# Attention scores of the array's two halves issued one by one instead of in pairs

## The chip, the cores and the metric

The kernel runs on one core of one Trainium2 chip. The metric is the device time of one execution in microseconds. A core has TensorE (PE in the profile; its weight loads are PEld), VectorE (DVE), ScalarE (ACT), GpSimd (POOL) and SyncE (SP), each with its own queue of instructions in order. They meet at semaphores. Matmuls write to PSUM, which has 8 banks of 512 fp32 columns on 128 partitions.

## The reference

One transformer layer with post-normalisation on x of 1024 tokens by 512:

```python
q = x @ Wq                      # 32 heads of 16
k, v = split(x @ Wkv)           # 8 groups of 16; 4 heads share a group
scores = q @ k.T                # causal: keys after the query are -inf
weights = softmax(scores / 4)
ctx = weights @ v
x = layernorm(x + ctx @ Wo + bo)
x = layernorm(x + x @ W.T + bias + lora(x))   # 8 adapters of rank 16, weighted
```

## The kernel before

**Units and cycles.** The sequence is cut into two halves of 512 queries (HT), and a unit is one half with one group: 4 heads, 16 units (NU). A unit's work on scores, exponentials and values is cut into *cycles*: one cycle takes 256 queries (s) and 256 keys, that is two key blocks of 128 (p). The first half has 3 cycles per unit, the second 7; 80 cycles in all. Cycle 24 is the first of the second half, and from there on the work repeats after two units, 14 cycles.

**Halves of the array.** A score matmul needs only 48 or 51 rows of the 128 (fp32 split in three terms of 16 rows, and three rows that carry the negated maximum). So two heads' pairs lie on two halves of the array's rows, partitions 0 to 63 and 64 to 127 (`tile_rows(t, ...)`, t = 0 or 1, PAIR = 2). Two matmuls that use different halves and different banks can run together.

**Pieces.** In each cycle, scores are computed in four *pieces*, each one bank: key block 0 on halves 0 and 1, then key block 1 on halves 0 and 1. The diagonal's second block is only 256 wide. The pieces' bank is `score_bank(e)`: three banks (3, 4, 5) go round up to piece 284 (cycle 71), six after that. ScalarE takes the exponential of each piece (L845) into PB. `bank_free(e)` makes TensorE wait until the exponential three pieces back is done. `accumulate(cyc - 1)` (L1300) then multiplies the previous cycle's probabilities by the values, in 16 small matmuls on bank 6. On diagonal cycles GpSimd masks PB first (L700).

**Chunks.** The maximum of each row must be known before the exponential, so the scores are also computed ahead with queries on the partitions: a *chunk* is one bank of such scores (L1118), for one block of 128 queries and one or two heads. VectorE reads it: a plain maximum where all keys are allowed (L897), or with the causal mask added (L904). 320 chunks in all, alternating between the array's halves: chunk n is on half n % 2. They use banks 0 to 2, and bank 7 when nothing else holds it; `CHUNK_BEHIND[n]` names the chunk or job that had the bank before, and `was_read` waits until it was read. When a unit's chunks are done, its maxima go through GpSimd, TensorE (`turn_maxima`, L1126), ScalarE and a DMA into three extra rows of QS, before the unit's first cycle.

**Order.** Everything is in an order written out ahead. The projections run first as jobs in three parts (`PLAN_A`), with the first 16 chunks between the parts. Then `DUE[c]` says how many chunks are due before cycle c; `level` computes it from costs, so that chunks are spread by the room that a cycle leaves on TensorE and VectorE. `chunks_of_cycle` cuts a cycle's lot in four quarters. TensorE's order within a cycle is: quarter 0, the pair of pieces 0 and 1, quarter 1, quarter 2, the pair of pieces 2 and 3, quarter 3, the cycle's *filler* if it has one, then `accumulate` of the cycle before. Fillers (`FILL`) are the late projections (Q, WE), transposes of the finished context (T1a, T1b, T2, T3) and the two output products (WO, FF). VectorE reads the chunks in the same order and does its part of the fillers after quarter 0. After cycle 79 a tail works off the last four blocks of tokens.

**Waits.** `max_scores` and `scores` each have one semaphore, raised once per pair by the last matmul of the pair. VectorE waits for pair n // 2 of `max_scores`, ScalarE for pair e // 2 of `scores`. SyncE waits for `scores` before it loads a new unit's queries into a slot of QS (5 slots, `load_queries`).

Of the kernel before, what the change touches and what calls it, by code (L numbers as in the profile page):

```python
# [18 lines left out]
def postln_kernel(nc, x, wq, wkv, wo, bo, lora_a, lora_b, w, bias, lora_w, xt, out):  # L19
# [120 lines left out]
    def chunks_of_job(n, part):  # L140

        before, due = PLAN_A[n - 1][1] if n else 0, PLAN_A[n][1]
        a, b = (before + (due - before) // 2 * p // 3 * 2 for p in (part, part + 1))
        return range(a, b)
# [48 lines left out]
    def level(chunks, cycles):  # L193

        total = COST[chunks[-1] + 1] - COST[chunks[0]]
        low, high = 0.0, 9.0
        for _ in range(40):
            ratio = (low + high) / 2
            room = [max(0.0, ratio * (0.4 * pe_time(c) + 1500) - 0.7 * dve_time(c)) for c in cycles]
            low, high = (low, ratio) if sum(room) > total else (ratio, high)  # L200
        done, due = 0.0, []
        for r in room:
            done += r
            due.append(2 * sum(1 for n in chunks[::2] if COST[n + 2] - COST[chunks[0]] <= done + 1))
        due[-1] = len(chunks)
        return [chunks[0] + d for d in due]
# [12 lines left out]
    def chunks_of_cycle(c):  # L219

        lot = range(DUE[c], DUE[c + 1])
        return [lot[len(lot) // 2 * q // 4 * 2:len(lot) // 2 * (q + 1) // 4 * 2] for q in range(4)]

# [70 lines left out]
    with ctx:  # L294
# [97 lines left out]
        qs_in = [sem(f"qs_in{s}") for s in range(SLOTS)]  # L392
        max_scores = sem("max_scores")
        max_read = sem("max_read")
# [4 lines left out]
        nm_in = sem("nm_in")  # L399
        scores = sem("scores")  # L400
        probs = sem("probs")
# [63 lines left out]
        def _(sp):  # L465
# [35 lines left out]
            def load_queries(u):  # L501
# [4 lines left out]
                if u >= SLOTS:  # L506
                    sp.wait_ge(scores, SCORE_BANKS[FIRST[u - SLOTS + 1]] // PAIR)
                parts_landed(PROJ.index(("Q", h, c)))
# [206 lines left out]
        def _(act):  # L715
# [120 lines left out]
            for cyc in range(NCYC):  # L836
# [4 lines left out]
                for k, (_, heads, skip) in enumerate(pieces(cyc)):  # L841
                    e = SCORE_BANKS[cyc] + k
                    width = len(heads) * (HQ - skip)
                    act.wait_ge(scores, e // PAIR + 1)
                    nc.scalar.activation(PB[:, cyc % NP_BUF, k, 0:width], PS[:, score_bank(e), 0:width], ACT.Exp,  # L845
# [35 lines left out]
        def _(dve):  # L881
# [7 lines left out]
            def chunk_max(n):  # L889
# [4 lines left out]
                bank = PS[:, CHUNK_BANK[n], :]  # L894
                dve.wait_ge(max_scores, n // PAIR + 1)
                if not own:
# [191 lines left out]
        def _(pe):  # L1088
# [7 lines left out]
            def chunk_scores(n):  # L1096

                u, qb, own, _ = CHUNKS[n]
                h, v = divmod(u, G)
# [12 lines left out]
                was_read(CHUNK_BEHIND[n])  # L1112
                was_read(CHUNK_BEHIND[n + 1])
                for k in range(len(CHUNKS[n][3])):
                    for t in range(PAIR):
                        j = CHUNKS[n + t][3][k]
                        rows = tile_rows(t, ROWS)
                        last = nc.tensor.matmul(PS[:, CHUNK_BANK[n + t], k * width:(k + 1) * width],  # L1118
                                                QS[rows, u % SLOTS, j % NPAIR, qb * P:(qb + 1) * P],
                                                KS[rows, v // 2, k0:k0 + width], start=True, stop=True)  # L1120
                last.then_inc(max_scores, 1)

# [134 lines left out]
            for n in range(NJOB_A):  # L1257
                for part in range(3):
                    pe_job(n, part)
                    for k in chunks_of_job(n, part)[::PAIR]:  # L1260
                        chunk_scores(k)
                    if JOBS[n] == ("V", 0, 0) and part == 1:
                        direct_queries()
                    if JOBS[n] == ("V", 1, 0) and part == 1:
                        turn_maxima(0)
# [52 lines left out]

            def pair_scores(cyc, i):

                u, s, _ = CYCLES[cyc]
                kb = key_blocks(cyc)[i]
                e = SCORE_BANKS[cyc] + PAIR * i
                for t in range(PAIR):
                    bank_free(e + t)
                for t in range(PAIR):
                    _, heads, skip = pieces(cyc)[PAIR * i + t]
                    rows = tile_rows(t, NROW)
                    last = nc.tensor.matmul(PS[:, score_bank(e + t), 0:len(heads) * (HQ - skip)],  # L1329
                                            KS[rows, (u % G) // 2, kb * P:(kb + 1) * P],  # L1330
                                            QS[rows, u % SLOTS, :, s * HQ + skip:(s + 1) * HQ], start=True, stop=True)
                last.then_inc(scores, 1)

            for cyc, (u, _, _) in enumerate(CYCLES):
                if cyc == FIRST[u]:
                    pe.wait_ge(nm_in, 16 * PAIR * (u + 1))
                for j, lot in enumerate(chunks_of_cycle(cyc)):
                    for n in lot[::PAIR]:
                        chunk_scores(n)
                    if j % 2 == 0:  # L1340
                        pair_scores(cyc, j // 2)
                    if cyc == rows_cycle(1) + 1 and j == 0:
                        turn_maxima(1)
                    filler(cyc, j)
# [73 lines left out]
```

## Time and profile before

| | us |
|---|---|
| median of 3 runs | 417.46 |
| lowest and highest run | 415.34, 418.66 |
| the profiled execution | 416.12 |
| its span in the profile | 414.4 |
| TensorE matmul busy | 337.4 (81%) |
| VectorE busy | 258.2 (62%) |
| ScalarE busy | 215.4 (52%) |
| GpSimd busy | 129.3 (31%) |

The span is the time from the first to the last instruction of the one profiled execution; its own measured time is 1.7 us longer. Matmuls are pipelined, so TensorE's busy time counts a matmul's latency too, and a share under 100% doesn't measure how much room is left. The idle time before an instruction is given with what ended it. The granted clock of TensorE was 0.887 of full speed on average over the span.

### The profile page before, as it was taken

What the parts mean: (1) busy time and instruction counts of PE and PEld (TensorE: products, weight loads), DVE (VectorE), ACT (ScalarE), POOL (GpSimd) and SP (SyncE); (2) the same over time, 40 slices, a digit from 0 to 9 for tenths busy, and PEclk for the clock granted to TensorE, in tenths of its full rate; (3) what the DMA queues carried; (4) which work ended last, traced back from release to release, by engine and by line L of the source; (5) the groups of instructions that cost most, each with busy time, mean ns of one, the idle gap of its engine ahead of it and who ended that gap; (6) DMA issues with size and microseconds to landing.
All of it is one profiled execution on the core that took longest, in us unless ns stands there. A gap on an engine that the chain in (4) does not pass through costs nothing.

```text
span 414.4 us, 7602 instructions
## 1 busy us (share of the span) xinstructions
PE 337.4 (81%) x2495; PEld 190.5 (46%) x2495; DVE 258.2 (62%) x783; ACT 215.4 (52%) x438; POOL 129.3 (31%) x292
## 2 busy tenths in 40 slices
PE   7986787877878887987878777788877876989994
PEld 3754454553543434433434434344343533546883
DVE  3455639457576556677687766878667775105664
ACT  4522425426345456566564755737647555595241
POOL 8730213222233335444512211321014112232353
PEclk9988568869897557599999989999899998899999
DMA  7766153832242101101001000000000000000002
GB/s 235 257 190 182 33 171 102 217 93 70 74 143 95 48 3 43 38 2 42 1 5 38 27 14 29 2 4 25 5 0 2 5 25 2 3 2 27 0 2 103
DMA packets 14198, 24.41 MB, mean 59 GB/s; under 512 B 2064, under 2 KB 4880, under 8 KB 14160
## 3 DMA queue, kind: packets, MB, share of 16 engines
q1 hardware_dynamic: 14160, 23.93, 18.8%
q8 instruction: 21, 0.34, 0.3%
q14 instruction: 17, 0.14, 0.1%
HBM read 16.19 MB, written 7.34 MB: 57 GB/s over the span
## 4 chain that ended last, share of the span: by engine, by line
PE 68%; ACT 10%; DVE 9%; issue 9%; DMA 1%; POOL 1%; SPq 0%; ACTq 0%; POOLq 0%; DVEq 0%
PE PS L1159 20%; PE PS L1300 18%; PE PS L1329 12%; PE PS L1118 10%; ACT PB L845 8%; DVE MX L897 4%; DVE scrap L904 4%; PE PS L1219 2%; PE PS L1227 2%; PE PS L1206 1%; DMA X<-in_L_attn_x_turned_dram 1%; ACT RAW L765 1%; DVE MX L904 1%; PE PS L1126 1%; PE PS L1132 0%
## 5 line engine op out<-in xcount | busy, mean ns | idle before, releaser
L845 ACT ACTIVATE PB<-PS 128x512 f32<-128x512 f32 (+1 forms) x320 | 159.3, 560 | 83.5 <-PE PS L1329 82.0
L904 DVE CUSTOM_DVE_ANT_0 scrap<-PS,mask 128x128 bf16<-128x128 f32 (+3 forms) x256 | 112.0, 487 | 37.8 <-PE PS L1118 36.5
L1329 PE MATMUL PS<-QS,KS 51*128 51x512 f32 (+1 forms) x320 | 80.1, 497 | 36.1 <-ACT PB L845 33.9
L700 POOL TENSOR_SCALAR_AFFINE_SELECT PB<-PB 128x256 f32<-128x256 f32 x128 | 50.2, 407 | 171.7 <-ACT PB L845 168.7
L897 DVE TENSOR_REDUCE MX<-PS 128x1 f32<-128x512 f32 x128 | 81.6, 684 | 35.3 <-PE PS L1118 34.8
L1118 PE MATMUL PS<-KS,QS 48*128 48x512 f32 (+3 forms) x384 | 75.4, 414 | 28.4 <-DVE MX L904 19.3
L1300 PE MATMUL PS<-PB,VX 128*32 128x256 f32 (+1 forms) x1280 | 87.7, 396 | 1.6 <-ACT RAW L765 0.8
L1329 PEld LDWEIGHTS PS<-QS,KS 51*128 51x128 f32 x320 | 34.7, 203 | 82.4 <-ACT PB L845 60.8
L1118 PEld LDWEIGHTS PS<-KS,QS 48*128 48x128 f32 x384 | 41.2, 207 | 49.8 <-DVE MX L904 28.0
L1300 PEld LDWEIGHTS PS<-PB,VX 128*32 128x32 f32 x1280 | 35.6, 116 | 44.0 <-issue 22.5
L1159 PE MATMUL PS<-XT,WQ 128*128 128x512 f32 x144 | 46.4, 478 | 1.0 <-ACT XT L810 0.8
L1159 PEld LDWEIGHTS PS<-XT,WQ 128*128 128x128 f32 x144 | 32.3, 234 | 12.8 <-issue 2.7
L765 ACT ACTIVATE RAW<-PS 128x256 f32<-128x256 f32 x32 | 12.4, 387 | 32.4 <-PE PS L1300 32.1
L736 ACT ACTIVATE parts<-PS 128x512 fp32r<-128x512 f32 x10 | 6.0, 597 | 36.0 <-PE PS L1159 36.0
L1159 PE MATMUL PS<-WQ,XT 128*128 128x512 f32 x96 | 24.2, 400 | 0.0
L1159 PE MATMUL PS<-XT 128*128 128x512 f32 x96 | 23.8, 398 | 0.0
L944 DVE TENSOR_TENSOR parts<-PS,parts 128x512 fp32r<-128x512 f32 x10 | 6.9, 691 | 24.0 <-ACT parts L736 24.0
L904 DVE DVE_READ_ACCUMULATOR2_ANT MX<- 128x1 f32 x256 | 21.2, 83 | 0.0
L680 POOL TENSOR_SCALAR mv<-mv 128x1 f32<-128x1 f32 x15 | 3.4, 227 | 56.9 <-DVE mv L993 56.9
L1159 PEld LDWEIGHTS PS<-WQ,XT 128*128 128x128 f32 x96 | 17.4, 188 | 4.8 <-DVE MX L897 1.0
L1159 PEld LDWEIGHTS PS<-XT 128*128 128x128 f32 x96 | 17.5, 188 | 4.2 <-issue 0.3
L662 POOL CAST NMPS<-NM 128x16 bf16<-128x16 f32 x15 | 3.3, 220 | 32.4 <-DVE NM L918 32.4
(87 smaller groups left out, 238.2 us busy)
## 6 DMA issues: line engine op xcount, KB each, us to landing
scr_q<-parts SPq DMA_DIRECT2D x8, 512.0 KB, 3.8
QS<-scr_q SPq DMA_DIRECT2D x30, 128.0 KB, 2.6
X<-in_L_attn_x_turned_dram SPq DMA_DIRECT2D x8, 256.0 KB, 6.4
X<-in_L_attn_x_dram SPq DMA_DIRECT2D x8, 256.0 KB, 2.9
out_dram<-TC SPq DMA_DIRECT2D x8, 256.0 KB, 2.0
QS<-scr_q SPq DMA_DIRECT2D x30, 64.0 KB, 2.5
scr_k<-parts SPq DMA_DIRECT2D x2, 512.0 KB, 3.7
RAW<-in_L_attn_Wo_dram SPq DMA_DIRECT2D x2, 512.0 KB, 4.7
```

The costliest lines, as they stand in the source:

```text
L700: nc.gpsimd.affine_select(out=blk, in_=blk, compare_op=ALU.is_ge, fill=0.0, base=0, pattern=[[0, len(heads)], [1, P]], channel_multiplier=-1)\
L765: nc.scalar.activation(RAW[:, u, cols], PS[:, PV_BANK, cols], ACT.Copy).then_inc(raw_out, 1)
L845: nc.scalar.activation(PB[:, cyc % NP_BUF, k, 0:width], PS[:, score_bank(e), 0:width], ACT.Exp, scale=SCALE).then_inc(probs, 1)
L897: nc.vector.tensor_reduce(part[:, j0:j1, 0:1], bank, AX, ALU.max).then_inc(max_read, 1)
L904: last = nc.vector.tensor_tensor_reduce(out=scrap[:, n % 2, (j - j0) * width:(j - j0 + 1) * width], in0=bank[:, j - j0, :], in1=mask[:, HT ...
L944: nc.vector.tensor_tensor(parts[:, s, 1, :], bank, parts[:, s, 0, :].bitcast(F32), ALU.subtract)\
L1118: last = nc.tensor.matmul(PS[:, CHUNK_BANK[n + t], k * width:(k + 1) * width], QS[rows, u % SLOTS, j % NPAIR, qb * P:(qb + 1) * P], KS[row ...
L1159: last = nc.tensor.matmul(bank, lhs(a, c), rhs(b, c), start=(k == 0), stop=(k == len(terms) - 1))
L1219: last = nc.tensor.transpose(bank[:, g * P:(g + 1) * P], RAW[:, h * G + g0 + g, qb * P:(qb + 1) * P], ident[:, :])
L1227: last = nc.tensor.transpose(bank[:, c * P:(c + 1) * P], src[:, c * P:(c + 1) * P], ident[:, :])
L1300: last = nc.tensor.matmul(PS[32 * j:32 * j + 32, PV_BANK, s * HQ + skip:(s + 1) * HQ], VX[:, key_blocks(cyc)[i], v_group(u, j), :], PB[:, ...
L1329: last = nc.tensor.matmul(PS[:, score_bank(e + t), 0:len(heads) * (HQ - skip)], KS[rows, (u % G) // 2, kb * P:(kb + 1) * P], QS[rows, u % ...
```

## The change

It cuts the schedule at single chunks instead of pairs of chunks, and at single pieces instead of pairs of pieces.

- A part of a projection job, a quarter of a cycle and the due table may hold an odd number of chunks.
- `max_scores` and `scores` become two semaphores each, one for each half of the array, raised by every chunk and by every piece. The readers wait for that of their half.
- `chunk_scores(n)` computes one chunk and waits for one bank; `piece_scores(cyc, k)` replaces `pair_scores(cyc, i)` in the same way.
- In each quarter there is now one piece. A variable `half` holds the half of the array that was used last: where the piece to come has that same half, the first chunk of the quarter goes ahead of it, the others behind it. The fillers stay whole, after the last quarter.
- `load_queries` waits for both semaphores of `scores`.

```diff
@@ chunks_of_job
-        a, b = (before + (due - before) // 2 * p // 3 * 2 for p in (part, part + 1))
+        a, b = (before + (due - before) * p // 3 for p in (part, part + 1))
@@ level
-            due.append(2 * sum(1 for n in chunks[::2] if COST[n + 2] - COST[chunks[0]] <= done + 1))
+            due.append(sum(1 for n in chunks if COST[n + 1] - COST[chunks[0]] <= done + 1))
@@ chunks_of_cycle
-        return [lot[len(lot) // 2 * q // 4 * 2:len(lot) // 2 * (q + 1) // 4 * 2] for q in range(4)]
+        return [lot[len(lot) * q // 4:len(lot) * (q + 1) // 4] for q in range(4)]
@@ semaphores
-        max_scores = sem("max_scores")
+        max_scores = [sem(f"max_scores{t}") for t in range(PAIR)]
-        scores = sem("scores")
+        scores = [sem(f"scores{t}") for t in range(PAIR)]
@@ load_queries
-                    sp.wait_ge(scores, SCORE_BANKS[FIRST[u - SLOTS + 1]] // PAIR)
+                    for t in range(PAIR):
+                        sp.wait_ge(scores[t], SCORE_BANKS[FIRST[u - SLOTS + 1]] // PAIR)
@@ ScalarE, the exponentials
-                    act.wait_ge(scores, e // PAIR + 1)
+                    act.wait_ge(scores[e % PAIR], e // PAIR + 1)
@@ VectorE, chunk_max
-                dve.wait_ge(max_scores, n // PAIR + 1)
+                dve.wait_ge(max_scores[n % PAIR], n // PAIR + 1)
@@ chunk_scores
                 was_read(CHUNK_BEHIND[n])
-                was_read(CHUNK_BEHIND[n + 1])
-                for k in range(len(CHUNKS[n][3])):
-                    for t in range(PAIR):
-                        j = CHUNKS[n + t][3][k]
-                        rows = tile_rows(t, ROWS)
-                        last = nc.tensor.matmul(PS[:, CHUNK_BANK[n + t], k * width:(k + 1) * width],
-                                                QS[rows, u % SLOTS, j % NPAIR, qb * P:(qb + 1) * P],
-                                                KS[rows, v // 2, k0:k0 + width], start=True, stop=True)
-                last.then_inc(max_scores, 1)
+                t = n % PAIR
+                rows = tile_rows(t, ROWS)
+                for k, j in enumerate(heads):
+                    last = nc.tensor.matmul(PS[:, CHUNK_BANK[n], k * width:(k + 1) * width],
+                                            QS[rows, u % SLOTS, j % NPAIR, qb * P:(qb + 1) * P],
+                                            KS[rows, v // 2, k0:k0 + width], start=True, stop=True)
+                last.then_inc(max_scores[t], 1)
@@ the projection jobs
-                    for k in chunks_of_job(n, part)[::PAIR]:
+                    for k in chunks_of_job(n, part):
                         chunk_scores(k)
@@ the cycles
-            def pair_scores(cyc, i):
+            def piece_scores(cyc, k):
                 u, s, _ = CYCLES[cyc]
+                i, heads, skip = pieces(cyc)[k]
                 kb = key_blocks(cyc)[i]
-                e = SCORE_BANKS[cyc] + PAIR * i
-                for t in range(PAIR):
-                    bank_free(e + t)
-                for t in range(PAIR):
-                    _, heads, skip = pieces(cyc)[PAIR * i + t]
-                    rows = tile_rows(t, NROW)
-                    last = nc.tensor.matmul(PS[:, score_bank(e + t), 0:len(heads) * (HQ - skip)],
-                                            KS[rows, (u % G) // 2, kb * P:(kb + 1) * P],
-                                            QS[rows, u % SLOTS, :, s * HQ + skip:(s + 1) * HQ], start=True, stop=True)
-                last.then_inc(scores, 1)
+                e = SCORE_BANKS[cyc] + k
+                bank_free(e)
+                rows = tile_rows(k % PAIR, NROW)
+                nc.tensor.matmul(PS[:, score_bank(e), 0:len(heads) * (HQ - skip)],
+                                 KS[rows, (u % G) // 2, kb * P:(kb + 1) * P],
+                                 QS[rows, u % SLOTS, :, s * HQ + skip:(s + 1) * HQ],
+                                 start=True, stop=True).then_inc(scores[k % PAIR], 1)
+            half = 0
...
                 for j, lot in enumerate(chunks_of_cycle(cyc)):
-                    for n in lot[::PAIR]:
+                    ahead = int(half == j % PAIR)
+                    for n in lot[:ahead]:
                         chunk_scores(n)
-                    if j % 2 == 0:
-                        pair_scores(cyc, j // 2)
+                    piece_scores(cyc, j)
+                    for n in lot[ahead:]:
+                        chunk_scores(n)
+                    half = lot[-1] % PAIR if lot[ahead:] else j % PAIR
```

## Rows read from the trace of the kernel before

**Rows 1.** The page's chain of waits that ended last: share by engine.

```profile
PE 68%; ACT 10%; DVE 9%; issue 9%; DMA 1%; POOL 1%; SPq 0%; ACTq 0%; POOLq 0%; DVEq 0%
```

**Rows 2.** Page, groups of instructions: busy us, mean ns | idle before, its releaser.

```profile
L904 DVE CUSTOM_DVE_ANT_0 scrap<-PS,mask 128x128 bf16<-128x128 f32 (+3 forms) x256 | 112.0, 487 | 37.8 <-PE PS L1118 36.5
L1329 PE MATMUL PS<-QS,KS 51*128 51x512 f32 (+1 forms) x320 | 80.1, 497 | 36.1 <-ACT PB L845 33.9
L897 DVE TENSOR_REDUCE MX<-PS 128x1 f32<-128x512 f32 x128 | 81.6, 684 | 35.3 <-PE PS L1118 34.8
L1118 PE MATMUL PS<-KS,QS 48*128 48x512 f32 (+3 forms) x384 | 75.4, 414 | 28.4 <-DVE MX L904 19.3
```

**Rows 3.** Stretches: length, busy us of five engines, PEclk, DMA share, GB/s.

```profile
130.00:170.00 40.00, 34.11 (x210) 15.03 (x212) 23.81 (x67) 20.43 (x46) 19.52 (x37) 0.59 0.18 59
185.80:189.60 3.80, 2.50 (x21) 1.39 (x20) 2.96 (x12) 2.44 (x5) 1.40 (x2) 1.00 0.02 6
225.41:280.12 54.71, 43.71 (x387) 22.78 (x387) 40.21 (x110) 33.02 (x67) 11.45 (x32) 0.97 0.04 14
```

**Rows 4.** Timeline of a quiet cycle: start us, us, instruction, [idle before].

```profile
203.07 0.19 PEld L1329 LDWEIGHTS PS<-QS,KS 51*128 51x128 f32 x2 [0.41 <-ACT PB L845]
203.07 0.50 PE L1329 MATMUL PS<-QS,KS 51*128 51x512 f32 x2
203.41 0.33 PE L1118 MATMUL PS<-KS,QS 48*128 48x384 f32 x2
204.41 0.39 PE L1329 MATMUL PS<-QS,KS 51*128 51x256 f32 x2 [0.67 <-ACT PB L845]
204.61 0.43 PE L1118 MATMUL PS<-KS,QS 48*128 48x512 f32 x2
204.97 1.07 PE L1300 MATMUL PS<-PB,VX 128*32 128x256 f32 x16
205.97 0.50 PE L1329 MATMUL PS<-QS,KS 51*128 51x512 f32 x2
```

**Rows 5.** Chain of waits in order of time, same cycle: start us, us, what.

```profile
203.67 0.61 ACT PB L845
204.28 0.14 issue
204.41 0.39 PE PS L1329 x2
```

**Rows 6.** Timeline of a cycle with three chunk pairs, TensorE's matmuls.

```profile
185.81 0.50 PE L1329 MATMUL PS<-QS,KS 51*128 51x512 f32 x2
...
187.42 0.44 PE L1118 MATMUL PS<-KS,QS 48*128 48x128 f32 x4 [0.88 <-DVE MX L897]
187.67 0.47 PE L1329 MATMUL PS<-QS,KS 51*128 51x512 f32 x2
188.56 0.51 PE L1118 MATMUL PS<-KS,QS 48*128 48x512 f32 x2 [0.42 <-DVE MX L904]
188.99 0.66 PE L1227 MATMUL PS<-ident,TC 128*128 128x128 f32 x4
```

**Rows 7.** Timeline, first piece pair and next work in three other such cycles.

```profile
193.52 0.51 PE L1329 MATMUL PS<-QS,KS 51*128 51x512 f32 x2
...
196.42 0.50 PE L1159 MATMUL PS<-WQ,XT 128*128 128x512 f32 x1
...
208.69 0.55 PE L1227 MATMUL PS<-ident,TC 128*128 128x128 f32 x3
...
213.17 0.50 PE L1329 MATMUL PS<-QS,KS 51*128 51x512 f32 x2
...
216.35 0.63 PE L1300 MATMUL PS<-PB,VX 128*32 128x256 f32 x6
```

**Rows 8.** Timeline at the lower clock: one cycle from piece pair to piece pair.

```profile
163.49 0.79 PE L1329 MATMUL PS<-QS,KS 51*128 51x512 f32 x2
...
167.87 0.79 PE L1329 MATMUL PS<-QS,KS 51*128 51x512 f32 x2
```

More of the change, by code:

```diff
@@ L1096, in chunk_scores @@
             def chunk_scores(n):
-                u, qb, own, _ = CHUNKS[n]
+                u, qb, own, heads = CHUNKS[n]
                 h, v = divmod(u, G)
```

## The prediction

> **What bounds the kernel now.** I read the page's chain of waits by engine first [rows 1]: the chain that ends last lies 68% on TensorE, 10% on ScalarE, 9% on VectorE, and 9% in "issue". TensorE sets the end, but not by arithmetic alone, so the next view is the groups of instructions with their idle times [rows 2]. The score matmuls of the cycles (L1329) waited 36.1 us for the exponentials (L845), and the score matmuls of the maxima (L1118) waited 28.4 us, mostly for VectorE's reads. At the same time VectorE's two readers (L904, L897) sat idle 37.8 and 35.3 us waiting for L1118. Two engines that wait for each other with three or four banks between them are a sign of lumps, not of a full engine. The table by stretch says the same [rows 3]: over one period of 14 cycles (54.71 us) TensorE is busy 43.71, VectorE 40.21, ScalarE 33.02.
>
> The timeline of one quiet cycle shows the loop [rows 4]. I call the two pieces' pair at 203.07 P0 and the one at 204.41 P1. P0 is followed by a chunk pair at 203.41, then TensorE has nothing for 0.67 us, P1 at 204.41, a chunk pair at 204.61, the value matmuls at 204.97, the next P0 at 205.97. P0 to P1 takes 1.34, P1 to the value matmuls 0.56, those 1.00 (to 205.97), and the cycle is 2.90. The chain shows why P1 stands still [rows 5]: its second bank (three banks go round) is freed by the exponential of P0's first piece, 0.61 us, and another 0.14 pass until P1 starts. P1's first bank had long been free.
>
> The second view is of cycles that hold three chunk pairs [rows 6]. From P0 at 185.81 to the work after the last chunk at 188.99 are 3.18 us, where the quiet cycle has 1.90: the chunk pair at 187.42 waited 0.88 for VectorE and the last one 0.42. VectorE was busy 2.96 of these 3.80 us [rows 3]. Pairs are issued only when both banks are read, so two chunks' matmuls come at once and VectorE then has a hole while the next pair is computed. I count 13 such cycles between cycle 29 and cycle 67 by the due table in the code: six like this one (3.18; another is 213.17 to 216.35), four with 205.97 to 208.69 (2.72), three with 193.52 to 196.42 (2.90) [rows 4, 6, 7].
>
> **The change, part by part.** I worked out both orders on paper from the due tables.
>
> *Slot after the last piece.* Score work can be cut at single chunks now. In 22 cycles (3, 6, 15, 17, and 18 from 28 to 68) the order was "P0, P1, chunk pair" or "..., P1, chunk pair"; it becomes "S0 S1 chunk chunk S2 S3 chunk". S2's bank is free already, so S2 runs in the gap where TensorE had nothing, and S3 alone waits for the exponential. The chunk behind S3 lies in the other half of the array, so it may start with S3 instead of after it. What is saved is one of the two slots between P1 and the value matmuls. A slot between successive users of the same half is 0.34 us (203.07 to 203.41) or 0.20 where the first is 256 wide (204.41 to 204.61) [rows 4]. I take 0.25: 22 x 0.25 = 5.5 us. The bounds are 0 (if something else then holds the value matmuls) and 22 x 0.34 = 7.5.
>
> *The other cycles.* In some 20 cycles (9 to 13, 20 to 27, 37 to 41, 51 to 55, about) the order becomes "S0 c S1 c S2 c S3 c", where each chunk has the same half as the piece ahead of it. Half 1 then carries S3 and a chunk in series after the release, 0.34 + 0.34 at most, which is what P1 and its chunk pair took. Ahead of S3 there are three steps of 0.34 in series and three starts on the opposite half. Two instructions of a pair start together in the rows of before (one row of x2, one start), so I take 0.02 for such a start: 1.02 + 0.06 = 1.08, inside the 1.34 that S3 waits anyway. Cost and gain are zero; the cover is 0.26 us. S1 comes 0.36 later than now, but its exponential has its turn only 0.5 + 0.6 us after S0, so that is covered too. S2's score is there earlier, which takes out ScalarE's hole between second and third exponential; it was not on the chain, since P1 to the value matmuls leaves room.
>
> *Stalls for VectorE.* The lots become single chunks, and the due table spreads them: the two-pair neighbours of heavy cycles go from 2 to 3 chunks, the heavy ones from 6 to 5 (nine of 13) or stay at 6 (the three before the output projection, and cycle 65). A third bank can be filled while two are unread. Over the quiet 1.90 the heavy cycles lose 1.28 (six), 0.82 (four) and 1.00 (three): 7.7 + 3.3 + 3.0 = 14.0 us in all. Removing one 0.68 us read of six, and the hole that a pair leaves, gives back, as my choice, 0.9 of 1.28 in six, 0.6 of 0.82 in three, and 0.3 in the four that keep six chunks: 5.4 + 1.8 + 1.2 = 8.4. Bounds: 0 and 14.0. What is late next there is VectorE itself, whose 40.21 us per period stay; 54.71 less this share (some 4) is 50.5, so it is at 80%, not the bound.
>
> *First 24 cycles.* Four cycles (2, 5, 8, 11) hold eight chunks and are near VectorE's own pace; I give them 0.4 each, 1.6. From cycle 71 on there are no chunks and six banks, so nothing changes; nor in the projections, except two or three chunks moved by one third of a job, hidden by VectorE's slack there (bounds -1 and +1).
>
> *What is added.* 320 more increments (640 for 320), the same number of bank waits, one more wait of the SP queue ahead of each query load, which is loaded four units ahead and hidden. The price of a satisfied wait with its bank is bounded by 204.41 to 204.61: 0.20 for a half whose weight load alone is 0.18 to 0.19, so at most 0.02 [rows 4]. One more such step per cycle lies behind the release, 60 x 0.02, about 1 us.
>
> The trace's own price for what follows a finished score matmul is the 0.14 us of issue in the chain, once per release and not per increment [rows 5]. The Trainium skill ("TensorE: Matmul & The Clock Gate", section "The cost: per-tile semaphore tail") speaks against this change: increments on concurrent tiles serialise, about 26 ns each, and one on the last tile suffices. By that rule, if all were on the path, an estimate of 320 x 0.026 = 8.3 us would be lost, and the sum below would come to about -6 instead of -14.5. Most of the increments fall where TensorE waits anyway, and the sum does not use it.
>
> Sum: -5.5 - 8.4 - 1.6 + 1.0 = **-14.5 us**. The profiled execution took 416.12 (span 414.4), 1.34 below the median; against the median of 417.46 the forecast is **403.0**.
>
> **Rivals.**
> *The halves do not run together across a wait (slower).* Today the partner follows with no wait between; in the new order a bank wait stands between any two. If an opposite-half start then costs a gap g instead of 0.02, the four-chunk cycles reach S3 after 1.02 + 3g; that exceeds the 1.34 from g = 0.11 on, and in three- and five-chunk cycles five serial steps exceed it from g = 0.27. With g = 0.34, fully serial: 20 x 0.70 + 31 x 0.36 = 25 us more; half of the VectorE gain is kept (4), the added step 1, so about 439. It cancels the whole gain at about g = 0.32, which is nearly serial. Against it: the 0.20 step with a satisfied wait in it. For it: no row shows an opposite-half start behind a wait. I give 0.12, with the smaller mishaps that end above 421.
>
> *The slack goes back to the release loop (no change).* P0 to S3 (1.34) stays, and VectorE keeps the heavy cycles at their length, because the chunk ahead of S1 or S2 now waits for a read and holds the piece behind it; before, its wait of up to 0.88 was partly covered by P1's. Then only part of the slots remain: 417.46 - 5.5 + 2 = 414. With weaker forms up to 421, chance 0.17.
>
> *The clock.* From 130 to 170 us the granted clock averages 0.59, that is mostly the 1.2 GHz level [rows 3]. A cycle at that level took 4.38 us (163.49 to 167.87) instead of 2.90 [rows 4, 8]. The stretch at half clock is worth about 40 x (1 - 2.90/4.38) x 0.8 = 11 us. Denser TensorE work could keep the 2.4 GHz level there and give 403 - 11 = 392; a second such stretch would cost as much, 414. Chance 0.11 for the better side.
>
> *It doesn't do what it says* has no room: the waits named are the ones the kernel issues.
>
> **How the numbers follow.** The forecast's own case, 397 to 409, has 0.60; no-change case 0.17 (414 to 421, of which about half lies within 1%, 413.3 to 421.6, with some of the main case's tail below); clock 0.11 (388 to 397); slower 0.12. About 1% is what a measurement of this kernel tells from no change. Faster by over 1%: 0.60 + 0.11 + 0.03 = 0.74; within 1%: 0.14; slower 0.12. The range 392 to 420 leaves out the slower rival (0.12) and the deeper half of the clock case (0.05).
>
> **What would show it.** In the profile after: L1118's idle before VectorE well under 28.4, VectorE's idle before L1118 down from 73; S3 alone at about 1.3 after S0 with S2 started inside that gap; in a three-chunk cycle the value matmuls 0.3 after S3 and the cycle at about 2.6; the T2, T3 and WO cycles shorter by 0.3 to 1.0; cycles from 71 on unchanged. Wrong if opposite-half neighbours start 0.2 or more apart, if S3's release drifts behind 1.4, if ScalarE's busy share approaches its limit, or if the half-clock stretch moves or grows.

## The result and the profile after

The changed kernel takes **378.19 us** (three runs, 377.22 to 378.72) against 417.46: a ratio of 0.906, 95% interval 0.900 to 0.913. Forecast were 403.0, with 392 to 420 as the range. The direction was right and the size was missed by a factor of 2.7: 39.3 us instead of 14.5. Its profiled execution has a span of 376.4 us and a mean granted clock of 0.941, where that of before had 414.4 and 0.887.

The groups of the page after, in the columns of [rows 2]; the lines have moved by one to three (L1326 is L1329 of before, L1117 is L1118, L905 and L898 are L904 and L897):

```profile
L905 DVE CUSTOM_DVE_ANT_0 scrap<-PS,mask 128x128 bf16<-128x128 f32 (+3 forms) x256 | 111.3, 486 | 30.9 <-PE PS L1117 30.4
L1326 PE MATMUL PS<-QS,KS 51*128 51x512 f32 (+1 forms) x320 | 104.9, 452 | 16.0 <-ACT PB L846 15.0
L1117 PE MATMUL PS<-KS,QS 48*128 48x512 f32 (+3 forms) x384 | 110.4, 388 | 7.1 <-DVE MX L905 4.8
L898 DVE TENSOR_REDUCE MX<-PS 128x1 f32<-128x512 f32 x128 | 81.7, 683 | 17.5 <-PE PS L1117 17.5
```

TensorE's waits for VectorE fell from 28.4 to 7.1 us, those for ScalarE from 36.1 to 16.0, VectorE's for TensorE from 73.1 to 48.4. Busy times of L1326 and L1117 rose (80.1 to 104.9 us, 75.4 to 110.4) though they do the same work: a matmul that starts alone is counted by itself, two that start together count once. The mean of one fell from 497 to 452 ns and from 414 to 388, so that rise is no cost.

The same cycle as in [rows 4] (cycle 33), TensorE's matmuls after the change:

```profile
180.29 0.44 PE L1117 MATMUL PS<-KS,QS 48*128 48x384 f32 x1
180.29 0.67 PE L1326 MATMUL PS<-QS,KS 51*128 51x512 f32 x2
180.64 0.56 PE L1117 MATMUL PS<-KS,QS 48*128 48x512 f32 x2
180.87 0.28 PE L1326 MATMUL PS<-QS,KS 51*128 51x256 f32 x1
181.54 0.38 PE L1326 MATMUL PS<-QS,KS 51*128 51x256 f32 x1 [0.35 <-ACT PB L846]
181.54 0.50 PE L1117 MATMUL PS<-KS,QS 48*128 48x512 f32 x1
181.97 1.07 PE L1299 MATMUL PS<-PB,VX 128*32 128x256 f32 x16
182.97 0.50 PE L1117 MATMUL PS<-KS,QS 48*128 48x512 f32 x1
182.98 0.73 PE L1326 MATMUL PS<-QS,KS 51*128 51x512 f32 x2
```

S0 to S3 are the four pieces of a cycle, each now issued by itself. The third piece (180.87) runs in the gap, the fourth (181.54) and a chunk of the other half start in the same hundredth, and the value matmuls follow after 0.43 instead of 0.56. S0 to S3 is 1.25 instead of 1.34, the cycle 2.69 instead of 2.90.

Heavy cycles are those with three chunk pairs before. The one from 213.17 [rows 7] had these two waits:

```profile
214.79 0.44 PE L1118 MATMUL PS<-KS,QS 48*128 48x128 f32 x4 [0.87 <-DVE MX L897]
215.92 0.50 PE L1118 MATMUL PS<-KS,QS 48*128 48x512 f32 x2 [0.41 <-DVE MX L904]
```

The same cycle after the change, with five chunks:

```profile
189.07 0.50 PE L1117 MATMUL PS<-KS,QS 48*128 48x512 f32 x1
189.07 0.73 PE L1326 MATMUL PS<-QS,KS 51*128 51x512 f32 x2
189.41 0.33 PE L1117 MATMUL PS<-KS,QS 48*128 48x128 f32 x2
189.58 0.45 PE L1326 MATMUL PS<-QS,KS 51*128 51x512 f32 x1
189.64 0.33 PE L1117 MATMUL PS<-KS,QS 48*128 48x128 f32 x2
190.34 0.49 PE L1326 MATMUL PS<-QS,KS 51*128 51x512 f32 x1 [0.32 <-ACT PB L846]
190.35 0.91 PE L1117 MATMUL PS<-KS,QS 48*128 48x512 f32 x2
191.18 1.07 PE L1299 MATMUL PS<-PB,VX 128*32 128x256 f32 x16
```

Both waits for VectorE are gone, and S0 to the value matmuls is 2.11 instead of 3.18.

The stretches show where 38 us of span went. I cut both traces at the same instructions:

| from, to (before; after) | before | after | saved |
|---|---|---|---|
| start to the projection at 54.21; 51.74 | 54.21 | 51.74 | 2.5 |
| to the projection at 121.60; 116.05 | 67.39 | 64.31 | 3.1 |
| to 132.20; 126.58 | 10.60 | 10.53 | 0.1 |
| to the transposes at 178.29; 157.87 | 46.09 | 31.29 | **14.8** |
| to the transposes at 334.36; 298.49 | 156.07 | 140.62 | **15.5** |
| to the end | 80.04 | 77.91 | 2.1 |

The fourth stretch, before and then after, and one period of 14 cycles after, in the columns of [rows 3]:

```profile
132.20:178.29 46.09, 39.53 (x261) 17.60 (x259) 27.88 (x77) 23.59 (x53) 18.75 (x37) 0.62 0.15 49
```

```profile
126.58:157.87 31.29, 29.23 (x259) 15.51 (x259) 26.74 (x78) 23.08 (x54) 19.53 (x38) 1.00 0.25 75
200.14:248.38 48.24, 44.70 (x388) 24.57 (x387) 39.33 (x111) 31.67 (x67) 11.30 (x32) 1.00 0.05 16
```

There the clock was 0.62 and is 1.00. The period has 48.24 us instead of 54.71, at about the same clock.

**Two parts, the clock and the rest.** In the experiments the kernel before took 405.9 to 432.2 us from one run to the next, most of it explained by the granted clock of each run; so times are compared at equal clock here. I call 2 x (1 - granted clock) x span the *half-clock time*, the time spent at 1.2 GHz instead of 2.4. Over 54 runs of the kernel before, it lies between 65 and 131 us, and the span follows 381.7 + 0.365 x half-clock time, with a scatter of 0.9 us. It is a line through whole runs: it does not say where in a run the clock fell. The profiled execution of before (93.7 us of it) lies at 380.2 when taken to zero, that of after (44.4) at 360.2. So about 20 us of the 38 are won at equal clock (22 against the line of the 54 runs), and 49 us less half-clock time give the other 18. The 94 us of before are near the middle of the 54 runs (96), so the 18 do not come from an unlucky run of before. That the slope of the kernel before holds for the other kernels is assumed. Within the runs of single kernels of ten runs it is 0.35 (pieces alone, chunks alone, table in twos) and 0.26 (idle matmuls in cycles 12 to 24); a slope smaller by 0.03 would turn the 22 into 23.5.

### The profile page after: what moved, and what is told of

It reads as the page before. It is cut to its first block, busy times and chain, and to the rows that moved or that the text cites. A ratio compares the mean times of both kernels' runs of the same rounds, so it can differ in the third digit from the quotient of the medians.

```text
span 376.4 us, 7312 instructions
## 1 busy us (share of the span) xinstructions
PE 339.1 (90%) x2495; PEld 198.7 (53%) x2495; DVE 252.9 (67%) x783; ACT 208.9 (56%) x438; POOL 128.5 (34%) x292
## 3 DMA queue, kind: packets, MB, share of 16 engines
q1 hardware_dynamic: 14160, 23.93, 20.5%
## 4 chain that ended last, share of the span: by engine, by line
PE 68%; ACT 13%; DVE 7%; issue 7%; DMA 2%; POOL 1%; SPq 0%; ACTq 0%; POOLq 0%; DVEq 0%
PE PS L1158 24%; PE PS L1299 19%; PE PS L1326 11%; ACT PB L846 10%; PE PS L1117 9%; DVE scrap L905 3%; DVE MX L898 2%; PE PS L1218 2%; ACT RAW L766 2%; PE PS L1226 2%; DMA X<-in_L_attn_x_turned_dram 2%; PE PS L1205 1%; DVE MX L905 1%; PE PS L1125 0%; ACT WQ L805 0%
## 5 line engine op out<-in xcount | busy, mean ns | idle before, releaser
L846 ACT ACTIVATE PB<-PS 128x512 f32<-128x512 f32 (+1 forms) x320 | 153.2, 566 | 60.6 <-PE PS L1326 60.3
L905 DVE CUSTOM_DVE_ANT_0 scrap<-PS,mask 128x128 bf16<-128x128 f32 (+3 forms) x256 | 111.3, 486 | 30.9 <-PE PS L1117 30.4
L1326 PE MATMUL PS<-QS,KS 51*128 51x512 f32 (+1 forms) x320 | 104.9, 452 | 16.0 <-ACT PB L846 15.0
L1117 PE MATMUL PS<-KS,QS 48*128 48x512 f32 (+3 forms) x384 | 110.4, 388 | 7.1 <-DVE MX L905 4.8
L898 DVE TENSOR_REDUCE MX<-PS 128x1 f32<-128x512 f32 x128 | 81.7, 683 | 17.5 <-PE PS L1117 17.5
L1299 PE MATMUL PS<-PB,VX 128*32 128x256 f32 (+1 forms) x1280 | 81.3, 373 | 1.7 <-ACT RAW L766 0.9
L1326 PEld LDWEIGHTS PS<-QS,KS 51*128 51x128 f32 x320 | 47.1, 189 | 56.2 <-ACT PB L846 44.5
L1117 PEld LDWEIGHTS PS<-KS,QS 48*128 48x128 f32 x384 | 58.4, 192 | 32.8 <-DVE MX L905 15.2
L1299 PEld LDWEIGHTS PS<-PB,VX 128*32 128x32 f32 x1280 | 34.0, 111 | 39.1 <-issue 16.6
L1158 PE MATMUL PS<-XT,WQ 128*128 128x512 f32 x144 | 47.9, 480 | 2.1 <-ACT XT L811 1.9
L1158 PE MATMUL PS<-XT 128*128 128x512 f32 x96 | 25.3, 417 | 1.0 <-DVE MX L905 0.8
L905 DVE DVE_READ_ACCUMULATOR2_ANT MX<- 128x1 f32 x256 | 21.2, 83 | 0.0
L784 ACT ACTIVATE TC<-RAW,shift,rstd 128x512 f32<-128x512 f32 x7 | 5.7, 817 | 13.4 <-POOL shift L683 13.4
```

Source lines behind the costliest of these rows:

```text
L898: nc.vector.tensor_reduce(part[:, j0:j1, 0:1], bank, AX, ALU.max).then_inc(max_read, 1)
L905: last = nc.vector.tensor_tensor_reduce(out=scrap[:, n % 2, (j - j0) * width:(j - j0 + 1) * width], in0=bank[:, j - j0, :], in1=mask[:, HT ...
L1117: last = nc.tensor.matmul(PS[:, CHUNK_BANK[n], k * width:(k + 1) * width], QS[rows, u % SLOTS, j % NPAIR, qb * P:(qb + 1) * P], KS[rows, v ...
L1158: last = nc.tensor.matmul(bank, lhs(a, c), rhs(b, c), start=(k == 0), stop=(k == len(terms) - 1))
L1299: last = nc.tensor.matmul(PS[32 * j:32 * j + 32, PV_BANK, s * HQ + skip:(s + 1) * HQ], VX[:, key_blocks(cyc)[i], v_group(u, j), :], PB[:, ...
L1326: nc.tensor.matmul(PS[:, score_bank(e), 0:len(heads) * (HQ - skip)], KS[rows, (u % G) // 2, kb * P:(kb + 1) * P], QS[rows, u % SLOTS, :, s ...
```

## The experiments

Each kernel's runs are reduced with the slope 0.365 and set against 381.7. "At equal clock" means that. "Table in twos" is the due table of before, in which an even number of chunks falls due in each cycle.

| kernel | median us | half-clock, median | against before at equal clock |
|---|---|---|---|
| changed | 378.2 | 44 | -22.0 |
| one wait per pair | 420.6 | 109 | -2.7 |
| pieces split alone | 410.4 | 83 | -3.4 |
| chunks split alone | 413.3 | 97 | -6.0 |
| both splits, old table and order | 404.4 | 83 | -9.7 |
| idle matmuls in cycles 12 to 24 | 410.4 | 77 | -0.4 |
| 320 more increments | 418.6 | 95 | +0.5 |
| changed, no chunk ahead | 376.4 | 41 | -22.1 |
| changed, table in twos | 412.0 | 98 | -6.6 |
| changed, table in twos in cycles 0 to 20 | 379.7 | 48 | -21.0 |
| changed, table in twos in cycles 21 to 69 | 399.9 | 66 | -7.6 |
| changed, idle matmuls in six early cycles | 388.1 | 41 | -9.8 |
| changed, value matmuls earlier | 367.4 | 50 | -34.1 |
| changed, idle matmuls in six early cycles and value matmuls earlier | 401.7 | 99 | -17.8 |

The scatter of a kernel's runs about its own value is 0.2 to 1.3 us, with three to ten runs each.

**One wait instead of two.** In the kernel before:

```diff
-                for t in range(PAIR):
-                    bank_free(e + t)
+                bank_free(e + 1)
```

> The kernel before, but a pair of pieces issues one bank wait (that of its second bank, which implies the first) instead of two. Theory A (a double wait ahead of a pair costs 0.10 us at each release: the chain had 0.14 us of issue before a released pair, 0.04 after the change): the issue falls to 0.04 and the time by about 0.10 x 70 cycles = 7, to 410. Rival B (the 0.10 comes from the second matmul of the pair or from the single semaphore of a piece, not from the wait): no change, 417.

The chain of this kernel in order of time, and the two piece pairs on its timeline:

```profile
256.17 0.60 ACT PB L845
256.77 0.04 issue
256.82 0.39 PE PS L1328 x2
```

```profile
255.57 0.50 PE L1328 MATMUL PS<-QS,KS 51*128 51x512 f32 x2
...
256.82 0.39 PE L1328 MATMUL PS<-QS,KS 51*128 51x256 f32 x2 [0.57 <-ACT PB L845]
```

The issue is 0.04 where it was 0.14 [rows 5], P0 to P1 1.25 where it was 1.34, and the cycle 2.80. Theory A holds for the mechanism: two waits ahead of a released instruction cost 0.10 more than one. The total is smaller than 7: 2.7 at equal clock. Most light and quiet cycles gained 0.08 to 0.10 each, a few nothing; the heavy cycles, which wait for VectorE, gave nothing (4.77 and 4.10 as before). The median was 420.6 because this kernel's runs had more half-clock time, 109 us.

**Pieces alone, chunks alone, both.** The change's code for the one, the other, and both, with the old due table and the old order (quarter 0, S0, S1, quarters 1 and 2, S2, S3, quarter 3).

```diff
-                    if j % 2 == 0:
-                        pair_scores(cyc, j // 2)
+                    if j % 2 == 0:
+                        piece_scores(cyc, j)
+                        piece_scores(cyc, j + 1)
```

```diff
-                    for n in lot[::PAIR]:
+                    for n in lot:
                         chunk_scores(n)
```

> The kernel before with pieces split alone: each piece waits for one bank and raises its half's semaphore; order, chunk pairs and due table stay. Theory A: S2 moves into the gap, the release costs 0.10 less per cycle, about -7 from that; the slot behind S3 is not saved because the chunk pair still follows as a pair; 410 if the half-clock stretch after 130 us stays, about 398 if the denser TensorE work removes it. Rival B (the gain of the change lies in the finer chunks): within 3 us of 417.

> The kernel before with chunks split alone: each chunk waits for one bank and raises its half's semaphore; order, piece pairs and due table (even numbers of chunks) stay. Theory A (finer bank use takes half of the VectorE stalls of 14 us in the heavy cycles): 410 with the half-clock stretch, 398 without. Rival B (VectorE's stalls come from the number of chunks in a heavy cycle, so only the due table helps): 415 to 417.

> The kernel before with pieces and chunks both split into single instructions with single waits, but with the order and the due table of before (chunks fall due in twos). Theory A (the splits alone carry the gain at equal clock): all cycles as after the change, quiet cycles 2.68, the heavy ones 3.70 and 3.11 instead of 4.77 and 4.18. Theory B (the first two runs suggest: single waits give 0.10 per cycle and 0.22 in some heavy cycles, the heavy cycles need the finer due table): quiet cycles 2.7 to 2.8, heavy ones 4.55 and 3.95; at equal clock about 9 us under the kernel before, where the change has 22.

Pieces alone, same cycle:

```profile
250.69 0.50 PE L1328 MATMUL PS<-QS,KS 51*128 51x512 f32 x2
251.03 0.34 PE L1119 MATMUL PS<-KS,QS 48*128 48x384 f32 x2
251.21 0.28 PE L1328 MATMUL PS<-QS,KS 51*128 51x256 f32 x1
251.93 0.38 PE L1328 MATMUL PS<-QS,KS 51*128 51x256 f32 x1 [0.45 <-ACT PB L846]
```

S2 starts in the gap, but S3 still comes 1.24 after S0, as with one wait. Moving S2 forward buys nothing by itself here: 3.4 us, hardly more than the single wait's 2.7. Chunks alone give 6.0: in the second half six heavy cycles fall from 4.77 to 4.55 and from 4.18 to 3.97, the ones of 4.10 not at all. The two add up (9.4; measured together 9.7). Theory B of the third expectation holds. So of the 22 us at equal clock more than half (12.3) is not in the splits.

**The order within the gap.** In the changed kernel:

```diff
-                    ahead = int(half == j % PAIR)
+                    ahead = 0
```

> The changed kernel, but every quarter issues its piece first and its chunks behind it, never one ahead. Theory A (the alternation of the halves lets neighbours start together): quiet cycles of three chunks become longer by up to 0.3 each, +5 to +10 in all. Rival (TensorE waits for the exponential anyway, the order within the gap is free): within 2 us of the changed kernel, heavy cycles at 3.7 to 3.1 as with the change.

The rival holds: 376.4, 22.1 at equal clock where the change has 22.0, and the cycles of 24 to 64 within 0.05 us of it. The rule that alternates the halves can go.

**The due table.** In the changed kernel, for all cycles, for 0 to 20, and for 21 to 69:

```diff
-            due.append(sum(1 for n in chunks if COST[n + 1] - COST[chunks[0]] <= done + 1))
+            due.append(2 * sum(1 for n in chunks[::2] if COST[n + 2] - COST[chunks[0]] <= done + 1))
```

> The changed kernel, but the due table again gives an even number of chunks to each cycle (2 and 6 where the change has 3 and 5); quarters still take single chunks. Theory A (the gain of 12 us at equal clock between the kernel with both splits and the changed kernel lies in moving one chunk out of the heavy cycles): heavy cycles back near 4.5 and 3.9 and 4.1, about +10 us, 386. Rival B (it lies in where the quarters put single chunks, S0 S1 c c S2 S3 c): heavy cycles near 3.8 with six chunks, within 4 us of the changed kernel.

> The changed kernel with the due table in even numbers for cycles 0 to 20 alone (eight-chunk and six-chunk cycles as before the change, four of six between cycle 14 and 19). Theory A (a cycle whose chunks come in a lump leaves TensorE waiting, the granted clock falls there and stays low for tens of us): a half-clock stretch of 20 us or more returns between 120 and 180 us, half-clock time rises from 44 to 70 or more, 376 becomes 388 to 395, with cycles 24 to 69 unchanged at 3.70, 3.11, 2.68 where the clock is full. Rival B (the stretch after 120 us has nothing to do with these lumps): half-clock time stays near 44 and the time rises by the stalls alone, 1 to 4 us.

> The changed kernel with the due table in even numbers for cycles 21 to 69 alone. Theory A: at equal clock the 13 heavy cycles cost 0.8 to 1.1 each again and the light ones up to 0.2, about +13; if lumps let the clock fall, half-clock time rises too, to 60 or more, and the time is 395 or more. Rival B (the fall of the clock belongs to the first 24 cycles only): half-clock time stays near 44, 388 to 391.

Cycle 36 with the table in twos in 21 to 69:

```profile
193.37 0.50 PE L1327 MATMUL PS<-QS,KS 51*128 51x512 f32 x2
193.70 0.57 PE L1118 MATMUL PS<-KS,QS 48*128 48x512 f32 x4
194.89 0.32 PE L1118 MATMUL PS<-KS,QS 48*128 48x128 f32 x1 [0.61 <-DVE MX L899]
...
195.48 0.91 PE L1118 MATMUL PS<-KS,QS 48*128 48x512 f32 x2
196.32 1.07 PE L1300 MATMUL PS<-PB,VX 128*32 128x256 f32 x16
```

With every split in place, six chunks in the cycle bring the stall back: 3.95 us for the cycle, where five chunks take 3.11. The first expectation's theory A holds for the mechanism: where the clock is full, the heavy cycles of the run with twos in all cycles are back at 4.55, 3.96 and 4.09. Its 386 us were missed (412.0), because the clock fell too.

In cycles 21 to 69 the table is the largest single part: 7.6 instead of 22.0 at equal clock, so 14.4 us. Where the clock is full, the table in twos costs about 0.8 in each heavy cycle, 1.0 in cycles 38 and 52 (four chunks where the change has three) and 0.1 to 0.2 in light ones. In the first 21 cycles the table is worth 1.0. The parts do not simply add: with the table in twos, the change's quarters and order are about 3 us behind the old ones (6.6 against 9.7 for both splits). Cycles 38 and 52 show part of it, 4.28 against 3.58.

The table moves the clock too: in twos, the median half-clock time is 98 us, in the late cycles alone 66; in single chunks it is 44, and 41 with no chunk ahead. Of the four runs with twos in cycles 0 to 20, three stayed at 44 to 48 and one went to 75 (390.0 us). The expectation of a fall after 120 us there was wrong in most runs: its profile has 6.8 us of it at 139 us, no more. The expectation for the late cycles held: 399.9, with lumps and more time at the lower clock.

**The clock by itself.** In the kernel before, ahead of the second pair in cycles 12 to 24:

```diff
+                    if j == 2 and 12 <= cyc < 25:
+                        bank_free(SCORE_BANKS[cyc] + 2)
+                        for _ in range(2):
+                            nc.tensor.matmul(PS[:, score_bank(SCORE_BANKS[cyc] + 2), :], Z[:, 0:P], Z[:, :], ...)
```

> The kernel before with two idle matmuls (zeros, 512 columns each, overwritten by the piece that follows) in the gap ahead of the second pair of pieces in cycles 12 to 24. Theory A (the change's 14.8 us between 132 and 178 us are mostly the half-clock stretch that was not entered): the granted clock from 130 to 178 rises from 0.62 to near 1.0 and the time falls by about 10, to 407. Rival B (the stretch is entered by other causes, or the time there is VectorE's): the clock stays near 0.6 and the time rises by up to 13 x 0.3 = 4.

The stretch of this kernel from 130 to 178 us, in the columns of [rows 3], where the whole of 130 to 170 had 0.59:

```profile
130.00:178.00 48.00, 40.77 (x377) 19.24 (x380) 38.09 (x106) 33.91 (x73) 24.21 (x48) 1.00 0.16 49
```

The clock stays full, and the profiled execution takes 405.1 us. One profile on each side proves little here: in the kernel with 320 more increments, which adds no work to the gaps, the same 130 to 178 us have 0.87. The runs carry it. All ten lie between 405.1 and 412.3, where the kernel before, measured beside them, lies between 405.9 and 432.2, and only 5 of its 25 runs are at 412.3 or below. The median is 5.8 lower, where about 10 was expected. With nothing else changed, filling the gaps took away the slow end; at equal clock it gives nothing (-0.4). So work in the gaps of these cycles can keep off a fall of the clock.

In the changed kernel the same was tried in cycles 1, 2, 5, 8, 11 and 14, where the clock still falls:

```diff
+                        if cyc in (1, 2, 5, 8, 11, 14):
+                            nxt = SCORE_BANKS[cyc] + j + 1
+                            bank_free(nxt)
+                            for _ in range(2):
+                                nc.tensor.matmul(PS[:, score_bank(nxt), :], Z[:, 0:P], Z[:, :], ...)
                         chunk_scores(n)
```

> The changed kernel with two idle matmuls (zeros, 512 columns, overwritten by the next piece) ahead of each chunk that follows a piece in cycles 1, 2, 5, 8, 11 and 14, where TensorE waits for VectorE and the granted clock falls at 42, 66, 83, 100 and 117 us. Theory A (waits of TensorE in these cycles let the clock fall, and the long projection behind them then runs at 1.2 GHz): half-clock time falls from 44 to under 20 us, and at 0.36 us per us of it the time by 9, less 2 for the added matmuls: 371. Rival B (the idle matmuls lie on the path): 378 to 382.

> The same idle matmuls in the kernel with the value matmuls ahead of the fourth piece (367.4 before this). Theory A: half-clock time from 50 to under 25 us, 360. Rival B: 367 to 371.

Both were slower: 388.1 instead of 378.2, and 401.7 instead of 367.4. From 39 to 67 us of the first, and from 67 to 119:

```profile
39.00:67.00 28.00, 26.68 (x82) 12.61 (x85) 11.06 (x45) 7.03 (x15) 4.05 (x12) 0.51 0.32 81
67.00:119.00 52.00, 49.61 (x364) 26.05 (x365) 33.86 (x144) 23.87 (x54) 14.43 (x45) 1.00 0.37 116
```

The clock was at 0.51 from 39 to 67 us. It fell at 39.3, before the first idle matmul (cycle 1 begins at 43.1), and the idle matmuls of cycles 1 and 2 then ran at the lower level: these two cycles took 7.9 and 17.5 us instead of 4.2 and 10.7, which is 10.4 of the 11.3 us that the kernel is late by cycle 24. Behind that the idle matmuls did what was expected of them. From 67 to 119 us the clock is 1.00, where the changed kernel has 0.87 from 65 to 117, and the falls at 66, 83, 100 and 117 us are gone from the profile. It gave no time: cycles 5, 8, 11 and 14 took 39.5 us together instead of 39.1, because the added matmuls cost what the clock gave. Half-clock time is 41 us, where the changed kernel has 44. So rival B holds, at a higher price than it had.

In the second kernel three of four runs had 96 to 103 us of half-clock time, one 47. Its profile has a stretch of 41 us at the lower clock from 153 us on, 22 us behind the last cycle with idle matmuls, where the kernel without them has none. What lets the clock fall in a given place stays open.

**Increments.** In the kernel before:

```diff
+                        if t == 0 and k == len(CHUNKS[n][3]) - 1:
+                            last.then_inc(extra, 1)
...
+                    if t == 0:
+                        last.then_inc(extra, 1)
```

> The kernel before with 320 more increments: the first matmul of every chunk pair and every piece pair raises a semaphore that nobody reads. Theory A (an increment is free unless somebody waits for it): quiet cycles stay at 2.90 and 1.34, no change at equal clock. Rival (increments on matmuls serialise at about 0.026 us each, an estimate from the Trainium skill's page TensorE: Matmul & The Clock Gate): quiet cycles 2.95 to 3.0, about +8 us.

```profile
249.00 0.50 PE L1332 MATMUL PS<-QS,KS 51*128 51x512 f32 x2
...
250.37 0.38 PE L1332 MATMUL PS<-QS,KS 51*128 51x256 f32 x2 [0.69 <-ACT PB L846]
...
251.93 0.50 PE L1332 MATMUL PS<-QS,KS 51*128 51x512 f32 x2
```

P0 to P1 grew from 1.34 to 1.37 and the cycle from 2.90 to 2.93. This cycle has two pairs of pieces and two of chunks, so four added increments lengthened it by 0.03, and by no more than its release. In all it came to 0.5 us at equal clock, too little to tell from zero. The Trainium skill ("TensorE: Matmul & The Clock Gate", section "The cost: per-tile semaphore tail") gives about 26 ns for one more increment on concurrent tiles. The trace agrees with that price where the increment stands ahead of a release (0.03, read to 0.01).

**A faster version.** In the changed kernel, the value matmuls of the cycle before go into the gap:

```diff
+                    if j == 3 and cyc:
+                        accumulate(cyc - 1)
                     piece_scores(cyc, j)
...
-                if cyc:
-                    accumulate(cyc - 1)
```

> The changed kernel with the value matmuls of the cycle before moved ahead of the fourth piece, into the gap in which that piece waits for the exponential. If the release loop (exponential, 0.04, S3, 1.00 us of value matmuls) is still what sets a quiet cycle: it falls from 2.68 to about 2.3 and VectorE or ScalarE (39.3 and 31.7 of 48.24 us per 14 cycles) comes next; about -10 us, to 367. Rival: the value matmuls hold S3 and with it the fourth exponential, and ScalarE's hole takes the gain back: within 3 us of 378.

It takes 367.4 us, ratio 0.899 (0.887 to 0.910) to the kernel before, measured beside it, and 34.1 less at equal clock, 12 more than the change. Eighty us of its middle:

```profile
200.00:280.00 80.00, 78.80 (x702) 43.85 (x703) 70.04 (x200) 58.54 (x122) 20.27 (x55) 1.00 0.05 14
```

VectorE is now busy 88% and TensorE nearly always. The shortest light cycles fell to between 1.9 and 2.1. Of the heavy ones, cycles 36 and 50, which have no filler, fell to 2.5; 29, 43, 48 and 67, which have one, stay at 3.2 to 3.4, and cycle 34 takes 4.6. TensorE's waits for VectorE come to 0.6 us in these 80, so VectorE is close to its limit but is not shown to be the bound.

## Why the prediction was wrong

*The release price.* The sum kept P0 to P1 at 1.34 because nothing in it seemed to change. But the 0.14 of issue in [rows 5] held 0.10 of the double wait, and the rows of before had no single wait to compare with. Measured: 1.25, in the cycles of 24 to 69 without a stall, and 1.25 with one wait per pair in the kernel before. The step "the other cycles: cost and gain are zero" failed by that: they gained 0.10 to 0.17. The 1.0 us put on for one more wait and increment behind the release did not show either, since S3 comes no later than with one wait. Not all cycles gained: the product cycle 37, which got a fifth chunk, grew from 5.85 to 6.04.

*The slot after the last piece* had the right mechanism and was somewhat over-sized. The light cycles went from 3.10 to 2.78 and cycle 33 from 2.90 to 2.68, but with both splits in the old order they already take 3.01 and 2.79. That leaves 0.11 to 0.23 for the slot, where 0.25 was taken. The mechanism shows where it is missing: with the table in twos in cycles 21 to 69, chunk numbers are even at each cycle's start, so that in cycle 33 the chunk behind S3 lies on S3's own half. It starts 0.23 after S3 (184.71, 184.94) instead of with it, the value matmuls follow after 0.55 instead of 0.43, and the cycle takes 2.79.

*The stalls for VectorE* were under-sized: 0.9, 0.6 and 0.3 per cycle taken, 1.07, 0.78 and 0.34 measured (4.77 to 3.70, 4.10 to 3.32, 6.65 to 6.31). Next to nothing of it is the wait's: with one wait these cycles took 4.77, 4.11 and 6.62. The cause was named rightly, and the table in twos in the changed kernel shows that in the cycles that go from six chunks to five most of it is that number, not the splits. Over cycles 24 to 69 I had some 12 us; the period of cycles 38 to 51, 54.71 to 48.24, less 1.3 for the clock's part in two of its cycles (5.85 and 3.19 instead of 4.77 and 2.94), gives 5.1 per 14 cycles, 17 in all.

*The first 24 cycles* were put at 1.6, plus 1.0 of slots. At equal clock about 22 less 17, 5 us, remain for them and the rest. The 1.6 were put in the wrong place: I gave them to the cycles with eight chunks, of which the first two did not get shorter (10.61 to 10.69, 10.44 to 10.87, part of each at the lower clock). Cycles 4 and 7, six chunks before and five after, fell at full clock from 3.97 to 2.74 and from 3.80 to 2.79.

*The clock* is the largest miss. I gave it no place in the sum and a rival with 0.11, sized from one 40 us stretch: 11 us. It was 18: the stretch from 130 us went entirely (14.8 us saved in that window, with the gains of its cycles), and the first long fall became shorter (13.7 us from 42.0 on, instead of 20.5 from 37.8 on). The row for it was there [rows 3, 8]. The price of a us at the lower level was nearly right, 0.34 from 1 - 2.90/4.38 against a slope of 0.365. The amount was not: the rival has 40 x 0.8, 32 us that could go, of the 94 in the profile, and 49 went. The error was to treat the lower clock as a given of the kernel, while the schedule moves it (98 us with the table in twos, 44 without), and to hold that rival against the main case instead of adding it. Rival and main case together, 392, would still have been 14 too slow.

*The slow rival*, halves that don't start together across a wait, did not occur: S3 and the chunk behind it start in the same hundredth (181.54), with a wait ahead of each. *The no-change rival*, a stall ahead of S1 or S2 that holds the pieces, did not occur either: S3 follows S0 by 1.25 to 1.27 in the heavy cycles too.

## What to carry to other kernels

Where two engines wait for each other through few banks, look at how evenly the work falls due as well as at how finely it is issued: here the splits with their single waits gave 10 us by themselves, and going back to a table in twos cost 14. Count the waits that stand ahead of a released instruction, and leave out those that a later one implies. And where a profile has stretches at the lower clock, price them as part of what a denser schedule may give back, with a slope from repeated runs, and expect the amount to be uncertain: why the clock falls where it does was not found here.

## What the runs showed of the hardware that I had not expected

- Two waits on the same semaphore ahead of a matmul cost about 0.10 us more at its release than one: 0.14 against 0.04 of issue, 1.34 against 1.25 from piece to piece.
- The same program ran between 405.9 and 432.2 us. The span followed the granted clock, 0.365 us for each us at 1.2 GHz, with a scatter of 0.9; the changed kernel's three runs and the four without the chunk ahead each lay within 1.5 us.
- Matmuls of the two halves of the array start in the same hundredth of a us (181.54) though each has its own wait ahead of it.
- Idle matmuls in the gaps kept the clock up where it had been full when they began: all ten runs at 412.3 or below with them in cycles 12 to 24, and, in one profile, 1.00 from 67 to 119 us with them in six early cycles. Where it had already fallen (0.51 from 39 to 67 us) they ran at the lower level and cost 10 us. What ends such a stretch is open.
